# A state-space layer's projection, norm, turn and gate: one stage ahead of the two directions, and an end by groups of four tiles

## What is computed

```python
def nbimamba2(x, ...):                       # x: layer-normed h, (64, 32, 128)
    h = layernorm(x @ pre_w + pre_b, pre_ln_g, pre_ln_b)         # 256 wide
    gate = silu(h)
    out_f = mamba2(h, ...f)                                      # 256 wide
    out_b = flip(mamba2(flip(h, 1), ...b), 1)
    out = layernorm((out_f * gate + out_b * gate) @ post_w + post_b, post_ln_g, post_ln_b)
    return out + x
def mamba2(...):  # projections, causal conv, scan over the tokens, silu gate, and at its end
    yn = yg * rsqrt(mean(yg * yg, -1) + 1e-5) * normw
    return yn @ wout
```

## Time and profile before

| | us |
|---|---|
| median of 3 runs | 3247.32 |
| lowest and highest | 3238.9, 3250.64 |
| the profiled execution, its own time | 3243.43 |
| the span of that execution's trace | 3241.6 |
| PE busy in the span (78%) | 2544.6 |
| DVE busy (73%) | 2352.4 |
| ScalarE busy (41%) | 1327.5 |
| POOL busy (44%) | 1419.5 |
| forward and backward direction together, 1657.4 to 2049.2 | 391.8 |

### The profile page before, as it was taken

How to read it: one execution, slowest core, us unless ns; L and a number is a source line. 1 busy time by engine, 2 the same in 40 slices (tenths; PEclk the granted TensorE clock), 3 DMA queues, 4 the chain that set the end, 5 groups by cost and what they waited for, 6 DMA issues and landing times. The chain is left out here.

```text
span 3241.6 us, 29207 instructions
## 1 busy us (share of the span) xinstructions
PE 2544.6 (78%) x8955; PEld 1510.7 (47%) x8955; DVE 2352.4 (73%) x3437; ACT 1327.5 (41%) x2109; POOL 1419.5 (44%) x897
## 2 busy tenths in 40 slices
PE   1778777677787772999857979479999659969599
PEld 0323222332332331666534837357777437733366
DVE  5699799759988976555557485658888548859566
ACT  2644444254454431222253343147776326730222
POOL 1499789649978971111123516110000310017266
PEclk9899889889999985999878989779999859979799
DMA  5155065116505410565300000022120011100021
GB/s 138 34 121 115 13 131 111 36 23 127 118 23 119 105 54 17 134 139 139 92 17 10 17 0 0 5 74 76 62 79 27 6 53 63 43 12 18 12 81 65
DMA packets 86604, 203.35 MB, mean 63 GB/s; under 512 B 12816, under 2 KB 25184, under 8 KB 77920
## 3 DMA queue, kind: packets, MB, share of 16 engines
q1 hardware_dynamic: 85952, 200.63, 24.6%
q0 software_dynamic: 512, 1.05, 0.1%
HBM read 198.76 MB, written 2.88 MB: 62 GB/s over the span
## 5 line engine op out<-in xcount | busy, mean ns | idle before, releaser
L532 DVE TENSOR_TENSOR m1x_HS<-m1x_R,m1x_HS 128x512 fp32r<-128x512 f32 x256 | 175.8, 691 | 69.2 <-ACT m1x_HS L500 64.9
L493 ACT ACTIVATE m1x_R<-m1x_ph,m1s_W 128x512 f32<-128x512 f32 x256 | 176.3, 689 | 107.2 <-PE m1x_ph L308 106.5
L1337 POOL TENSOR_TENSOR t2x_KM<-t2x_KT,t2x_HM 128x2048 f32<-128x2048 f32 x8 | 28.8, 3603 | 432.7 <-ACT t2x_KT L1410 416.0
L1688 POOL TENSOR_TENSOR t3xs_QH<-t3xs_HS,t3xa_Q 128x512 f32<-128x512 f32 x64 | 81.0, 1266 | 287.9 <-DVE t3xs_HS L1672 287.9
L829 DVE TENSOR_TENSOR m0x_T<-m0x_S,m0x_pb 128x512 f32<-128x512 f32 x128 | 88.1, 689 | 131.3 <-PE m0x_pb L308 131.2
L815 ACT ACTIVATE m0x_S<-m0x_pa 128x512 f32<-128x512 f32 x128 | 76.5, 598 | 214.2 <-PE m0x_pa L308 214.2
L2117 PE MATMUL t0x1fs_acc<-t0x1fs_HC,g_ident 128*128 128x512 f32 x256 | 133.6, 654 | 38.6 <-POOL t0x1fs_HC L2198 38.5
L2117 PE MATMUL t0x0fs_acc<-t0x0fs_HC,g_ident 128*128 128x512 f32 x256 | 133.2, 651 | 38.3 <-POOL t0x0fs_HC L2198 38.2
L2117 PE MATMUL t0x1bs_acc<-t0x1bs_HC,g_ident 128*128 128x512 f32 x256 | 131.2, 641 | 39.3 <-POOL t0x1bs_HC L2198 39.2
L2117 PE MATMUL t0x0bs_acc<-t0x0bs_HC,g_ident 128*128 128x512 f32 x256 | 130.2, 639 | 35.7 <-POOL t0x0bs_HC L2198 35.6
L2198 POOL TENSOR_TENSOR t0x1bs_HC<-t0x1bs_HS,t0x1bs_CB 128x1024 f32<-128x1024 f32 x64 | 149.1, 2360 | 10.7 <-DMA t0x1bs_CB<-t0x1b_bc_rows 4.2
(11 more groups left out here) (915 smaller groups left out, 7637.6 us busy)
## 6 DMA issues: line engine op xcount, KB each, us to landing
m0x_GS<-m_gate_rows SPq DMA_DIRECT2D x64, 512.0 KB, 6.6
t0x0fs_CB<-t0x0f_bc_rows SPq DMA_DIRECT2D x32, 512.0 KB, 6.3
t0x0bs_CB<-t0x0b_bc_rows SPq DMA_DIRECT2D x32, 512.0 KB, 6.5
t0x1fs_CB<-t0x1f_bc_rows SPq DMA_DIRECT2D x32, 512.0 KB, 6.4
t0x1bs_CB<-t0x1b_bc_rows SPq DMA_DIRECT2D x32, 512.0 KB, 6.6
m1x_GS<-m_gate_rows SPq DMA_DIRECT2D x16, 1024.0 KB, 4.7
m1s_W<-in_L_w SPq DMA_DIRECT2D x16, 514.0 KB, 3.3
m2x_GS<-m_gate_rows SPq DMA_DIRECT2D x8, 1024.0 KB, 4.7
```

Of the source, the lines that this page charges most:

```text
L493: a.activation(R[:, s % 4, :], ph[s % 4][:, :], ACT.Relu, bias=W[:, e % RAW, weights.cut + c:weights.cut + c + 1]).then_inc(relu_ready, 1)
L532: v.tensor_tensor(HS[:, s % 4, 1, :], R[:, s % 4, :], HS[:, s % 4, 0, :].bitcast(F32), ALU.subtract).then_inc(low_made, 1)
L1337: nc.gpsimd.tensor_tensor(KM[:, i % 2, :, :], keys, spread(HM[:, :], W), ALU.mult).then_inc(km_made, 1)
L1688: nc.gpsimd.tensor_tensor(QH[:, s % 4, :], HS[:, s % 4, :], Q[:, c], ALU.mult).then_inc(read, 1)
```

## The change

The front. The stages t1xp, t1xpl and t1xpt become one. DVE takes the four statistics of a group right after the group's bias addition. The normalise is shared out by tiles: even ones on ScalarE, odd ones on DVE. PE turns the normalised rows, still without gamma and beta, group by group, into the PSUM banks in which the projection lay. Gamma and beta are now applied as the turned rows leave PSUM: features lie on the partitions there, so they are one scale and one bias per partition, on ScalarE for features 0 to 127 and on DVE for 128 to 255. They are loaded as two columns each, laid out so in DRAM. `GATE` is gone.

The end. The stages t1xo, t1xot and t1xq become one, which works by groups. ScalarE scales a tile of `OU[0]`; DVE scales that of `OU[1]` and adds it in one instruction; PE turns the sum; ScalarE takes the silu of the group's columns in `HT` in place; DVE multiplies the turned sum, from PSUM, into them; PE projects the group; DVE adds the bias two groups later. The wait for all four loads now stands ahead of the first sum on DVE and of the first transpose on PE.

`turn_256` is no longer called and is removed. The layer norm at the end and both directions are unchanged.

```diff
-            GB = sp_.sb("GB", [P, 2, 256])
+            GB = sp_.sb("GB", [P, 2, 2])
             PRE = sp_.sb("PRE", [P, TILES, 256])
-            psum = Stage(nc, name + "pp")
-            psum.__enter__()
-            pp = psum.ps("pp", [P, TILES, 256])
+            m = moment_tiles(sp_, TILES)
+            stats, mean, var, rstd = m["stats"], m["mean"], m["var"], m["rstd"]
+            shift = sp_.sb("shift", [P, TILES])
+            pp = sp_.ps("pp", [P, TILES, 256])
...
-                    sp.dma_start(GB[:, 0, :], w["pre_ln_g"].partition_broadcast(P)).then_inc(loaded, 16)
-                    sp.dma_start(GB[:, 1, :], w["pre_ln_b"].partition_broadcast(P)).then_inc(loaded, 16)
+                    sp.dma_start(GB[:, 0, :], w["pre_ln_g"]).then_inc(loaded, 16)
+                    sp.dma_start(GB[:, 1, :], w["pre_ln_b"]).then_inc(loaded, 16)
...
+
+                def bank(k):
+                    return pp[:, 2 * k:2 * k + 2, :].rearrange("p t c -> p (t c)")
 
                 @block.tensor
                 def _(pe):
                     pe.wait_ge(loaded, 96)
                     for t in range(TILES):
                         pe.matmul(pp[:, t, :], XT[:, t * P:(t + 1) * P], WP[:, :], start=True, stop=True).then_inc(made, 1)
+                    for g in range(GROUPS):
+                        for c in range(2):
+                            for t in range(g * GT, (g + 1) * GT):
+                                if t % 2:
+                                    pe.wait_ge(odd_made, t // 2 + 1)
+                                else:
+                                    pe.wait_ge(even_made, t // 2 + 1)
+                                mm = pe.transpose(bank(2 * g + c)[:, (t % GT) * P:(t % GT + 1) * P],
+                                                  PRE[:, t, c * P:(c + 1) * P], ident[:, :])
+                            mm.then_inc(turned, 1)
 
...
                     for g in range(GROUPS):
                         s = slice(g * GT, (g + 1) * GT)
                         dve.wait_ge(made, (g + 1) * GT)
-                        nc.vector.tensor_tensor(PRE[:, s, :], pp[:, s, :], PB[:, :].unsqueeze(1).broadcast_to([P, GT, 256]),
-                                                ALU.add)
-
-            psum.__exit__(None, None, None)
-            layer_norm(nc, name + "pl", PRE, TILES, 256, GB, 1e-5)
-            turn_256(nc, name + "pt", PRE, HT, ident, GATE)
+                        v.tensor_tensor(PRE[:, s, :], pp[:, s, :], PB[:, :].unsqueeze(1).broadcast_to([P, GT, 256]),
+                                        ALU.add).then_inc(biased, 1)
+                        dve.wait_ge(biased, g + 1)
+                        for t in range(g * GT, (g + 1) * GT):
+                            last = v.bn_stats(stats[:, t, :], PRE[:, t, :])
+                    link(last)
+                    moments(nc, link, m, TILES, 256, 1e-5).then_inc(var_ready, 1)
+                    dve.wait_ge(root_ready, 1)
+                    link(v.reciprocal(rstd[:, :], rstd[:, :]))
+                    v.scalar_tensor_tensor(shift[:, :], mean[:, :], -1.0, rstd[:, :], ALU.mult, ALU.mult).then_inc(rstd_ready, 1)
+
+                    def evict(g):
+                        dve.wait_ge(turned, 2 * g + 2)
+                        v.tensor_scalar(HT[:, 1, g * GROUP:(g + 1) * GROUP], bank(2 * g + 1), GB[:, 0, 1:2], GB[:, 1, 1:2],
+                                        ALU.mult, ALU.add)
+
+                    for g in range(GROUPS):
+                        for t in (g * GT + 1, g * GT + 3):
+                            v.tensor_scalar(PRE[:, t, :], PRE[:, t, :], mean[:, t:t + 1], rstd[:, t:t + 1],
+                                            ALU.subtract, ALU.mult).then_inc(odd_made, 1)
+                        if g:
+                            evict(g - 1)
+                    evict(GROUPS - 1)
+
+                @block.scalar
+                def _(act):
+                    act.wait_ge(var_ready, 1)
+                    nc.scalar.activation(rstd[:, :], var[:, :], ACT.Sqrt).then_inc(root_ready, 1)
+                    act.wait_ge(rstd_ready, 1)
+
+                    def evict(g):
+                        act.wait_ge(turned, 2 * g + 1)
+                        nc.scalar.activation(HT[:, 0, g * GROUP:(g + 1) * GROUP], bank(2 * g), ACT.Identity,
+                                             bias=GB[:, 1, 0:1], scale=GB[:, 0, 0:1])
+
+                    for g in range(GROUPS):
+                        for t in (g * GT, g * GT + 2):
+                            nc.scalar.activation(PRE[:, t, :], PRE[:, t, :], ACT.Identity, bias=shift[:, t:t + 1],
+                                                 scale=rstd[:, t:t + 1]).then_inc(even_made, 1)
+                        if g:
+                            evict(g - 1)
+                    evict(GROUPS - 1)
...
-                    link = Chain(dve, chain)
-                    dve.wait_ge(root_made, 2)
-                    link(v.reciprocal(RT[:, :, :], RT[:, :, :]))
-                    for d in range(2):
-                        link(v.tensor_tensor(OU[d][:, :, :], OU[d][:, :, :], spread(RT[:, d, :], 256), ALU.mult))
-                    link(v.tensor_tensor(OU[0][:, :, :], OU[0][:, :, :], OU[1][:, :, :], ALU.add))
-                    link(v.tensor_tensor(OU[0][:, :, :], OU[0][:, :, :], GATE[:, :, :], ALU.mult))
-
-            turn_256(nc, name + "ot", OU[0], HT, ident)
             with Stage(nc, name + "q") as sq:
+                turned = [sq.ps(f"turned{i}", [P, 2, GROUP]) for i in range(2)]
...
+                    @block.scalar
+                    def _(act):
+                        for d in range(2):
+                            nc.scalar.activation(RT[:, d, :], MS[d][:, :], ACT.Sqrt).then_inc(root_made, 1)
+                        act.wait_ge(rt_ready, 1)
+                        for g in range(GROUPS):
+                            for t in range(g * GT, (g + 1) * GT):
+                                nc.scalar.activation(OU[0][:, t, :], OU[0][:, t, :], ACT.Copy,
+                                                     scale=RT[:, 0, t:t + 1]).then_inc(scaled, 1)
+                            s = slice(g * GROUP, (g + 1) * GROUP)
+                            nc.scalar.activation(HT[:, :, s], HT[:, :, s], ACT.Silu).then_inc(silu_made, 1)
+
...
+                        v = nc.vector
+                        dve.wait_ge(root_made, 2)
+                        v.reciprocal(RT[:, :, :], RT[:, :, :]).then_inc(rt_ready, 1)
+                        dve.wait_ge(rt_ready, 1)
+
+                        def gate(g):
+                            s = slice(g * GROUP, (g + 1) * GROUP)
+                            dve.wait_ge(silu_made, g + 1)
+                            dve.wait_ge(turn_made, g + 1)
+                            v.tensor_tensor(HT[:, :, s], HT[:, :, s], turned[g % 2][:, :, :], ALU.mult).then_inc(gated, 1)
+
+                        def bias(g):
+                            s = slice(g * GT, (g + 1) * GT)
+                            dve.wait_ge(made, g + 1)
+                            v.tensor_tensor(Y[:, s, :], po[:, s, :], GB[:, 2, :].unsqueeze(1).broadcast_to([P, GT, P]), ALU.add)
+
+                        dve.wait_ge(loaded, 64)
+                        for g in range(GROUPS + 1):
+                            if g < GROUPS:
+                                for t in range(g * GT, (g + 1) * GT):
+                                    dve.wait_ge(scaled, t + 1)
+                                    v.scalar_tensor_tensor(OU[0][:, t, :], OU[1][:, t, :], RT[:, 1, t:t + 1], OU[0][:, t, :],
+                                                           ALU.mult, ALU.add).then_inc(summed, 1)
+                            if g:
+                                gate(g - 1)
+                            if g >= 2:
+                                bias(g - 2)
+                        bias(GROUPS - 1)
+
                     @block.tensor
...
+                        def project(g):
+                            pe.wait_ge(gated, g + 1)
+                            for t in range(g * GT, (g + 1) * GT):
+                                for k in range(2):
+                                    mm = pe.matmul(po[:, t, :], HT[:, k, t * P:(t + 1) * P], WO[:, k, :],
+                                                   start=(k == 0), stop=(k == 1))
                             mm.then_inc(made, 1)
...
+                        pe.wait_ge(loaded, 64)
                         for g in range(GROUPS):
+                            if g >= 2:
+                                pe.wait_ge(gated, g - 1)
+                            for t in range(GT):
+                                pe.wait_ge(summed, g * GT + t + 1)
+                                for c in range(2):
+                                    mm = pe.transpose(turned[g % 2][:, c, t * P:(t + 1) * P],
+                                                      OU[0][:, g * GT + t, c * P:(c + 1) * P], ident[:, :])
+                            mm.then_inc(turn_made, 1)
```

(3 more changed lines are left out.)

78 lines of the change are left out of this document (29 added, 49 removed).

## The result

The changed kernel took 3199.86 us (median of 4; 3198.04 to 3207.42), the kernel before, beside it on the same chip, 3244.16 (4; 3238.90 to 3250.64). The ratio is 0.987, with a 95% interval of 0.985 to 0.989. The prediction said 3210 of 3247.3, which is 0.9885.

A forecast was written before the change was run, and what follows sets the result against it. No engine fills the span; in the front and the end one engine works at a time. Savings of 22.1 + 2.0 + 13.7 = 37.8 us take the median 3247.3 to 3210 us, range 3199 to 3224.

The forecast's parts named there:

- (a): Front: statistics taken under the projection, DVE setting the pace; moments start at 1625.4 instead of 1627.68, 2.3 us saved.
- (b): Front, normalise, turn and evict: three engines overlap, 7.85 us plus 0.3 barrier; direction starts at 1635.3, 22.1 us saved.
- (c): Forward direction's first 64 tiny matmuls: run at higher clock after shorter PE standstill; 2 us saved, bounds 0 and 3.4.
- (d): End: DVE and PE wait for four loads, taking 3.7 us, until 2054.2; each microsecond beyond is paid in full.
- Rival 2: End's loads land late; half a microsecond likely, only 12 us more takes the kernel to 3222; chance 0.06.
- (e): End, DVE's work from 2054.2: sums 6.4, gates 4.8, bias additions 2.6, together 13.8 us.
- (f): End, ScalarE from 2051.3: scalings 6.4, silu 3.9, table load 1.28, 11.6 us in all; stays ahead of DVE after two groups.
- (g): End: PE needs 13.0 us; walking the queues, last bias addition ends at 2070.7 with 2.7 of waits, 13.7 us saved.
- (h): Layer norm after the end: a table load of 1.28 us ahead of its root, hidden within 5 us.
- rival 1: PE stays at half clock through the end: 6.8 us saved there, 29 to 31 in all, 3217; chance 0.16.
- (3): Clock stays at half through a direction's recurrent loop, work growing by up to 100 us; 3264 or more; chance 0.02.
- (4): Front and end: waits string the engines out as before; 15 us saved, 3232; chance 0.03.

The follow-up runs named there:

- e1: The changed kernel run once more, unaltered: 3204.90 us, ratio 0.988 to the kernel before.
- e5: Against the changed kernel, all 16 statistics taken behind the last bias addition, in the same stage: 3209.92 us in one run.
- e2: The new end alone, on the kernel before, with the GATE taken out of the front: 3221.52 us, ratio 0.993.
- e4: Against the changed kernel, the end's four loads issued in the front, into buffers that live through the layer: 3198.07 us in one run.
- e10: On top of e4, the silu made in one instruction at the start of the backward direction's recurrent loop: 3204.58 us in one run.
- e8: Against the changed kernel, transposes that nobody reads added on idle PE, 44 behind the projection and 34 ahead of the end's turns: 3193.15 us in one run.
- e7: Against the changed kernel, the end's sums made as two wide operations a group instead of four narrow ones: 3210.25 us in one run.
- e9: Against the changed kernel, both directions' 64 tiny matmuls moved behind the convolution's first four units, 16 each: 3189.51 us, ratio 0.983.
- e6: Against the changed kernel, ScalarE normalises all 16 tiles and VectorE keeps its evictions: 3204.62 us in one run.

## Why the prediction came out

The mechanism was the one foreseen: stages in which one engine worked at a time became one in which three do, and the gain lies in the two stretches named. The profiled executions differ by 36.0 us where 37.8 was forecast; that of e1 differs by 38.6. The medians differ by 44.3 and 40.5. The layer's start alone moved by up to 11 us from one execution to another, so these agree. Part of the closeness is luck: in the first profile the front and the end gave 2.3 us more than their terms, and the forward direction 2.7 less. Step by step:

(a) 12.69 us from first addition to moments became 10.39: 2.3 saved, as said; e5 gave 2.0 of it back.

(b) 8.16 us from normalise to the direction, said 8.15. Inside it sizes were off and cancelled: VectorE's eviction took 0.81 us, not 0.69, its tile 0.36, not 0.41, PE's turns with their waits 6.38, not 6.3, at 0.50 for the most part, and the last eviction followed the last turn more closely than by 0.25. VectorE stood still for 1.47 us ahead of its first eviction; the prediction had named such a wait as a sign of being wrong, but PE's turns went on beside it and it cost nothing. The stage as a whole began its projection 1.0 us sooner (5.44 behind the first DMA issue, not 6.43): the prediction held the start fixed, though the two loads for gamma and beta, now small, left room, and the last load landed in 3.1 us instead of 4.1. The runs bear this out: e2, which keeps the two large loads, kept 11.6 us to the projection and 4.1 to the landing, and each run with the small ones and the same wait had 10.2 to 10.7. In sum 23.1, not 22.1.

(c) Near in its mean, wrong as a fixed term. Over the nine executions whose direction code is the changed kernel's, the forward direction took 87.3 to 91.6, on average 89.2, and 90.4 and 91.1 in the two with the old front. That is 1.6 less, against the 2 of the sum, but both old ones lie inside the spread of the nine, so a saving is not shown. But in the profile of the changed kernel itself it lost 0.7, outside the bounds of 0 and 3.4. The step that failed took a clock read in one execution for one that comes each time.

(d) "Paid in full" failed. The loads landed in 2.9 us, not 3.7, and e4 took the wait away altogether and the end stayed at 20.1. In e2 they took 3.7 and the first sum came 0.5 us later, and the end was 20.2. Rival 2's price rests on the same sentence. Loads later than in e2 were not tried, so where their cost begins stays open.

(e) VectorE's work: sums 1.67 for four (0.40 and a little each), gates 1.22, bias additions 0.69. Added up these are 14.3, but neighbours overlap by some 0.1 us each; VectorE was busy for 13.7 of the 15.5 us from the first sum on, against 13.8.

(f) "It stays ahead of DVE after two groups" failed in the case that mattered, the second group: with 1.70, 1.28, 1.06 and 1.69 us in ScalarE's queue, the second group's scalings are done 5.7 us after the first one's start. e4 and e10 showed that this sets the pace up to the first gate once the loads are early, 2.4 us of the end. With the loads in the end the two waits end within 0.25 us of each other, so each hides the other.

(g) First sum to last addition's end: 15.5 instead of 16.5. The term that was mis-sized is the waits: VectorE's holes came to 1.8 us, not 2.7. The clock rose a little later than it was taken to rise, during the first projection. The end saved 15.0, not 13.7, though (d) puts the earlier landing at next to nothing. The alternative of "full clock throughout, 14.9" was not what made it so: in e8 the first turns at 1.00 moved nothing.

(h) Hidden, as said: the table load stands 0.3 us behind the last bias addition, and ScalarE's root comes 5.3 us behind the first statistic in both. From the last bias addition to the next layer took 16.1 us instead of 15.7; the 0.3 stand at the next layer's first instruction, and e2, which has the table load too, took 15.8.

No rival happened: 1.00 from 2038.3 (rival 1), loads in 2.9 us (2), 0.94 in the loop (3), and rows of several engines at once (4).

Of the two rules, neither showed here. ScalarE's scaling ended at 2030.15, the load stands from 2030.17 to 2031.45 and the silu starts at 2031.46. The drain of 1.38 us that the Trainium skill gives in "ScalarE: Activation LUTs", "What ACT_TABLE_LOAD costs", has no room there. And e7, with half as many sums, took 3.0 us more, against the Trainium skill's "VectorE: DVE Perf Modes", "Rules for kernel authors", taken by itself: it says to keep the number of operations low, and here the fewer operations passed twice the elements.

## What to carry to other kernels

A chain of stages in which one engine works at a time can give more than any engine's busy time suggests (36.0 us here, where no engine lost more than 13); price the merged stage by its longest queue plus head and tail, and walk each queue to its second group, where a table load or a moved operation shows. When two waits end close together, removing one gives nothing until the other is gone (e4, then e10). Small matmuls in a row, which others wait for, belong among PE's work while its partners are busy rather than ahead of it: in e9 they added 4 us or less to the convolution instead of 10 to 12, 10 to 15 us less by the medians.

## What the runs showed of the hardware

The granted clock at the same place of the same program differed between executions. The 64 matmuls of 8 columns took 12.4 us once and 10.6 once, and 9.8 to 13.6 over the runs with the same code there. PE was busy without a hole in both (for 12.42 of 12.42 us and 10.56 of 10.56), and yet the clock fell from 1.00 to 0.50, once after 1.4 us and once after 3.4; what decides when is open. The 13.6 are those of e6, where PE's turns ahead had had holes and the clock stood at 0.50 from the first tiny matmul. In e8 PE worked for 5.0 us at 1.00, stood still for 2.8, and the clock then averaged 0.64 over the first 3.4 us of the turns; with 34 transposes ahead of the end's turns, and 1.3 us of standing still between, it was 1.00 for the first group and 0.56 for the second.

A VectorE TENSOR_SCALAR of 128x512 from PSUM with two operands read per partition took 0.81 us each time, where a TENSOR_TENSOR of that size from PSUM takes 0.69. The same kind of operation between buffers in SBUF, 128x256, took 0.36 us, where the prediction's pace for two tensors gave 0.41. ScalarE's table load took 1.28 us, and the silu began 1.31 us after the scaling ahead of the load had ended.
